# Mixture-of-experts tail of a fused block: 45 slots of 128 rows become 25 full slots and 14 slots shared by two experts

## The reference, cut to what matters

```python
# x, ctx: (32, 128, 256) f32; 16 heads of 16; 14 experts; hidden width 512
x = x + tanh(g_xattn) * attention(layernorm(x), ctx, ctx)     # causal, biases on q, k, v and dense
h = layernorm(x).reshape(4096, 256)
logits = h @ router_w                                         # (4096, 14)
e = argmax(logits); weight = softmax(logits)[e]
hid = gelu(h @ w1[e] + b1[e])                                 # (512,)
x = x + tanh(g_ffn) * weight * (hid @ w2[e] + b2[e])
```

## Time and profile before

| | |
|---|---|
| median of three runs | 489.14 us (488.89 to 490.43) |
| profiled execution, its own time | 491.46 us |
| its span | 489.6 us |
| busy in the span: TensorE, its weight loads, VectorE, ScalarE, GpSimd | 96%, 83%, 70%, 64%, 65% |
| mean granted TensorE clock | 0.991 of full speed |
| moved by DMA | 73.05 MB |

### The profile page before, as it was taken

How to read it: one execution, slowest core, us unless ns; L and a number is a source line. 1 busy time by engine, 2 the same in 40 slices (tenths; PEclk the granted TensorE clock), 3 DMA queues, 4 the chain that set the end, 5 groups by cost and what they waited for, 6 DMA issues and landing times.

```text
span 489.6 us, 17052 instructions
## 1 busy us (share of the span) xinstructions
PE 471.0 (96%) x4871; PEld 408.1 (83%) x4872; DVE 344.8 (70%) x1108; ACT 312.6 (64%) x1450; POOL 317.3 (65%) x686
## 2 busy tenths in 40 slices
PE   8999999999999999999999998989899999999991
PEld 4888888888888888888888887879799999999991
DVE  3678999999999999999999997654344334334431
ACT  2589899889898898898898897442222332233230
POOL 5465577686776777777777676686655555655621
PEclk9899999999999999999999999999999999999997
DMA  7264565312312212213111057598988888878810
GB/s 232 75 236 142 168 196 158 72 52 57 75 44 60 69 43 70 59 46 83 44 56 55 26 170 220 155 241 289 293 265 279 264 271 281 286 262 264 269 39 0
DMA packets 37904, 73.05 MB, mean 149 GB/s; under 512 B 12761, under 2 KB 21471, under 8 KB 37856
## 3 DMA queue, kind: packets, MB, share of 16 engines
q1 hardware_dynamic: 24752, 32.13, 22.8%
q10 hardware_dynamic: 6048, 23.54, 14.9%
q0 software_dynamic: 7056, 16.79, 11.1%
HBM read 59.06 MB, written 15.07 MB: 151 GB/s over the span
## 4 chain that ended last, share of the span: by engine, by line
PE 74%; ACT 7%; DVE 5%; DMA 4%; issue 3%; POOL 2%; SPq 1%; ACTq 0%; POOLq 0%; DVEq 0%
PE bank L1323 14%; PE bank L1314 14%; PE bank L1354 10%; PE bank L1423 9%; ACT arena L760 7%; PE bank L1413 5%; PE bank L1346 5%; PE bank L1491 5%; PE bank L1362 4%; DMA g_rows<-token_rows,fetch_idx 3%; PE bank L1301 2%; PE bank L1409 2%; DVE negmax L982 2%; PE bank L1341 2%; DMA arena<-ctxt 2%
## 5 line engine op out<-in xcount | busy, mean ns | idle before, releaser
L760 ACT ACTIVATE arena<-bank,negmax 128x128 f32<-128x128 f32 x512 | 179.6, 403 | 13.4 <-DVE negmax L982 13.4
L744 ACT ACTIVATE hid_t<-bank,w_ring 128x128 f32<-128x128 f32 x180 | 51.3, 369 | 114.5 <-PE bank L1314 90.2
L760 ACT ACTIVATION_READ_ACCUMULATOR arena<-bank,negmax 128x1 f32 x512 | 124.1, 242 | 0.0
L982 DVE TENSOR_REDUCE negmax<-bank 128x4 f32<-128x512 f32 x128 | 84.6, 683 | 9.6 <-PE bank L1346 8.9
L1314 PE MATMUL bank<-g_xt,w_ring 128*128 128x128 f32 x720 | 87.9, 275 | 0.6 <-DVE g_xt L955 0.6
L1323 PE MATMUL bank<-W,hid_t 128*128 x360 | 85.4, 380 | 1.6 <-ACT hid_t L744 0.8
L1314 PEld LDWEIGHTS bank<-g_xt,w_ring 128*128 128x128 f32 x720 | 84.6, 192 | 1.5 <-issue 1.0
L971 DVE SCALAR_TENSOR_TENSOR g_out<-bank,g_name,g_out 128x256 f32<-128x256 f32 x45 | 21.8, 484 | 86.5 <-PE bank L1323 86.5
L1354 PE MATMUL bank<-C,arena 128*128 128x128 f32 x512 | 78.9, 277 | 2.5 <-ACT arena L760 1.9
L1323 PEld LDWEIGHTS bank<-W,hid_t 128*128 128x128 f32 x360 | 65.0, 190 | 9.4 <-issue 2.4
L1423 PE MATMUL bank<-arena 128*128 128x128 f32 x512 | 71.5, 283 | 0.5 <-DMA arena<-ctxt 0.3
(11 more groups left out here) (151 smaller groups left out, 774.4 us busy)
## 6 DMA issues: line engine op xcount, KB each, us to landing
w_ring<-w1b ACTq DMA_DIRECT2D x35, 642.0 KB, 5.0
token_rows<-rows SPq DMA_DIRECT2D x32, 256.0 KB, 3.6
W<-w SPq DMA_DIRECT2D x14, 512.0 KB, 4.9
w_ring<-w1b SPq DMA_DIRECT2D x10, 642.0 KB, 7.2
arena<-x SPq DMA_DIRECT2D x32, 128.0 KB, 2.0
arena<-ctxt SPq DMA_DIRECT2D x31, 128.0 KB, 2.7
slot_names<-token_names SPq DMA_DIRECT2D x45, 1.0 KB, 4.6
g_rows<-token_rows,fetch_idx POOLq DMA_INDIRECT x45, 4.5
```

The lines of the kernel that those rows point to most:

```text
L744: ins = act.activation(hid_t[:, RING[k], ch, :], hid_bank[k][:, ch * P:(ch + 1) * P], ACT.Gelu, bias=w_ring[:, k, B1_AT + ch:B1_AT + ch + 1])
L760: ins = act.activation(probs[:, q, v, :], bank[q][:, v * P:(v + 1) * P], ACT.Exp, bias=negmax[:, b.par, h:h + 1], accum_out=rsum[:, b.par, ...
L982: dve.tensor_reduce(negmax[:, b.par, q * HQ:(q + 1) * HQ], bank[q][:, :].rearrange("p (v k) -> p v k", v=HQ), axis=AX_X, op=ALU.max, negat ...
```

## The change: full and mixed slots

A slot still has 128 rows, but there are 25 full ones (`FULL`) for one expert each, and then 14 mixed ones (`MIXED`), 39 in all. In mixed slot j, rows 0 to 63 are a half of any expert (from a table), and rows 64 to 127 are the last half tile of expert j, the same for every run.

- In a mixed slot the tokens are stationary and the weights move. `half_up`: for each of 2 chunks, one matmul of 64 stationary columns and 512 moving ones for the upper half (weights in `w_ring`) and one for the lower half (weights in the new resident `W1`), into partitions 0 to 63 and 64 to 127 of bank 5. `hidden` copies the bank (128 x 512) to `u_sb`, `turn` transposes it (4 transposes), `half_gelu` is 8 activations of 64 columns, `half_down` 4 x 2 matmuls of 64 stationary and 256 moving columns.
- `W1`, 512 KB for each of 14 experts, takes the place of the attention's buffers; SyncE loads it between slots 5 and 30 (`load_resident`). `load_half` issues three transfers for a mixed slot instead of one. Names of a mixed slot come in two transfers.
- `normed_rows` is gone from every batch step. `rows` holds 256 values, mean and reciprocal deviation (258 floats), and is stored when `rstd2_ready` is given. VectorE normalises gathered rows (`norm`, one slot further ahead than `up_in`), and `up_in` reads `g_xn`.
- The tables: `remaining_tiles` counts half tiles (6 linked operations where there were 2), and `take_full`, `half_tiles`, a second `place` and `half_lines` follow slots 11 to 14.
- The hardware loops over slots are written out, so all indices and waits there are constants.

```diff
-SLOTS = (TOK - E) // P + E
+HALF = P // 2
+MIXED = E
+FULL = (TOK // HALF - 1 - MIXED + 1) // 2
+SLOTS = FULL + MIXED
-ROW = 2 * D
+ROW = D + 2
...
+            def load_resident(e, behind):
+                hold(base_ready, behind)
+                sp.dma_start(W1[:, e, :], w1b[e, :, 0:DC * F]).then_inc(resident_loaded[e], 16)
...
+            load_resident(0, 5)
             for r in range(4):
                 hold(name_stored[r], 16 * (B // 4) + 16)
             hold(tables_ready, 2)
+            for s in range(EARLY, FULL):
+                hold(names_loaded[s % R], 16 * (s // R))
+                load_names(s % R, s)
+            load_resident(1, 9)
+            load_resident(2, 12)
+            load_resident(3, 15)
+            hold(tables_ready, 3)
+            for s in range(FULL, SLOTS):
+                hold(names_loaded[s % R], 16 * transfers(s - R, 2))
+                load_half_names(s % R, s)
+            for e in range(4, E):
+                load_resident(e, 18 + 2 * (e - 4) if e < 7 else 17 + e)
...
+            def load_half(r, s):
+                j = s - FULL
+                ex = act.value_load(half_expert[0:1, j:j + 1], min_val=0, max_val=E - 1)
+                weights = w1b[bass.ds(ex, 1), :, :].rearrange("e p n -> (e p) n")
+                act.dma_start(w_ring[:, r, 0:B2_AT], weights[:, 0:B2_AT]).then_inc(up_loaded[r], 16)
+                act.dma_start(w_ring[0:HALF, r, B2_AT:UPW], weights[0:HALF, B2_AT:UPW]).then_inc(up_loaded[r], 16)
+                act.dma_start(w_ring[HALF:P, r, B2_AT:UPW], w1b[j, HALF:P, B2_AT:UPW]).then_inc(up_loaded[r], 16)
...
+            def half_in(s):
+                half_gelu(s)
+                if s + R < SLOTS:
+                    hold(hid_t_ready, s + 1)
+                    hold(base_ready, s + 1)
+                    load_half(s % R, s + R)
...
+            def norm(r, s):
+                dve.wait_ge(rows_fetched[r], s // R * 16 + 16)
+                wait(dve, gx_transposed, s - 1)
+                dve.tensor_scalar(g_xn[:, RING[r], :], g_rows[:, r, 0:D], g_rows[:, r, MEAN:RSTD], g_rows[:, r, RSTD:ROW],
+                                  ALU.subtract, ALU.mult).then_inc(gx_normed, 1)
...
+            def full_slot(s):                      # VectorE
+                start_out(s % R, s)
+                up((s + 2) % R, s + 2)
+                norm((s + 3) % R, s + 3)
+                if s == FULL - 2:
+                    hidden(FULL)
+                    up((s + 3) % R, s + 3)
+                result(s % R, s)
+            def mixed_slot(s):                     # VectorE
+                if s + 3 < SLOTS:
+                    norm((s + 3) % R, s + 3)
+                start_out(s % R, s)
+                if s + 2 < SLOTS:
+                    hidden(s + 2)
+                if s + 3 < SLOTS:
+                    up((s + 3) % R, s + 3)
+                result(s % R, s)
...
-            def normed_rows(h):
-                normed(h, rows[:, h.slot, 0:D], rows[:, h.slot, D:2 * D], moments2, rstd2, rstd2_ready, h_ready)
...
             for s in range(4, EARLY):
+                norm((s + 3) % R, s + 3)
                 result(s % R, s)
...
+            def half_up(s):
+                j = s - FULL
+                pe.wait_ge(gx_ready, s + 1)
+                wait(pe, hidden_ready, j)
+                pe.wait_ge(up_loaded[s % R], 16 * transfers(s, 3))
+                pe.wait_ge(resident_loaded[j], 16)
+                for ch in range(DC):
+                    cols = slice(ch * F, (ch + 1) * F)
+                    pe.matmul(bank[5][0:HALF, :], g_xt[:, RING[s % R], ch, 0:HALF], w_ring[:, s % R, cols],
+                              start=(ch == 0), stop=(ch == DC - 1))
+                    ins = pe.matmul(bank[5][HALF:P, :], g_xt[:, RING[s % R], ch, HALF:P], W1[:, j, cols],
+                                    start=(ch == 0), stop=(ch == DC - 1))
+                ins.then_inc(half_hid_done, 1)
+            def half_down(s):
+                pe.wait_ge(hid_t_ready, s + 1)
+                pe.wait_ge(out_ready, s - 1)
+                ex = pe.value_load(half_expert[0:1, s - FULL:s - FULL + 1], min_val=0, max_val=E - 1)
+                for ch in range(FC):
+                    pe.matmul(y_bank[s % R][0:HALF, 0:D], hid_t[:, RING[s % R], ch, 0:HALF],
+                              W2[:, bass.ds(ex, 1), ch, :].rearrange("p e n -> p (e n)"),
+                              start=(ch == 0), stop=(ch == FC - 1))
+                    ins = pe.matmul(y_bank[s % R][HALF:P, 0:D], hid_t[:, RING[s % R], ch, HALF:P], W2[:, s - FULL, ch, :],
+                                    start=(ch == 0), stop=(ch == FC - 1))
+                ins.then_inc(y_done, 1)
+            def mixed_slot(s):                     # TensorE
+                if s + 2 < SLOTS:
+                    half_up(s + 2)
+                if s + 1 < SLOTS:
+                    turn(s + 1)
+                if s + 3 < SLOTS:
+                    up_in((s + 3) % R, s + 3)
+                if s < FULL:
+                    down(s % R, s)
+                else:
+                    half_down(s)
```

More of the change, by code:

```diff
@@ L1228, in _ @@
             row_moments(batch(30))
+            norm(2, 2)
             up(2, 2)
@@ L1243, in _ @@
             up(3, 3)
-            start_out(1, 1, 0)
+            start_out(1, 1)
             choose(last)
+            norm(4, 4)
             result(1, 1)
-            normed_rows(last)
             up(4, 4)
-            start_out(2, 2, 0)
+            start_out(2, 2)
             take_early()
@@ L1270, in _ @@
             up(1, EARLY + 1)
-            with dve.Fori(2, SLOTS // R - 1) as i:
-                for k in range(R):
-                    slot(k, i * R + k, i)
-            for k in range(R):
-                slot(k, SLOTS - R + k, SLOTS // R - 1, ahead=k + 2 < R)
+            for s in range(EARLY, FULL - 1):
+                full_slot(s)
+                if s == EARLY + 1:
+                    take_full()
+                if s == EARLY + 2:
+                    half_tiles()
+                if s == EARLY + 3:
+                    place(t_key_base, HALF)
+                if s == EARLY + 4:
+                    half_lines()
+            for s in range(FULL - 1, SLOTS):
+                mixed_slot(s)
         @block.tensor
@@ new lines, in full_slot @@
+            def full_slot(s):
+                up_in((s + 2) % R, s + 2)
+                up((s + 1) % R, s + 1)
+                if s == FULL - 2:
+                    half_up(FULL)
+                    up_in((s + 3) % R, s + 3)
[6 more added lines that the diff above has]
+                if s + 3 < SLOTS:
+                    up_in((s + 3) % R, s + 3)
+                if s < FULL:
+                    down(s % R, s)
+                else:
+                    half_down(s)
```

322 lines of the change are left out of this document (192 added, 130 removed).

## The result

The kernel before measured 489.25 us (median of 8, 488.44 to 491.34), the changed kernel 485.93 us (median of 8, 484.69 to 489.22). The ratio is 0.9921, 95% interval 0.9896 to 0.9946: 3.3 us less, where 7.8 us less was forecast. The time lies inside the range. The profiled execution of the changed kernel has a span of 484.0 us and an own time of 485.86.

What follows compares the result with a forecast made beforehand. TensorE, busy 96% of the span, was taken as the bound. 489.6 - 74.8 (full slots) + 62.6 (mixed slots) + 0.5 (end) + 1.5 (DMA) + 2.5 (joint) = 481.9 us span; median 0.46 below, 481.4 us; range 475 to 490.

Steps and rivals of the forecast that it cites:

- the mixed slot: TensorE's time for one slot of two halves, 4.47 us; 14 of them 62.6 us.
- the step that everything hung on: In `half_up` and `half_down`, both column groups work at once, so each takes 1.73 us, half of 3.46.
- both rivals on overlap: Mixed slots: groups overlap only in part, 490.4 us, chance 0.05; or not at all, 530 us, chance 0.03.
- ScalarE and the gathers stay hidden in the mixed slots: ScalarE occupied 4.4 of 4.47 us, gathers landing in time; rivals: gathers pace, 486, chance 0.12; ScalarE paces, 497, 0.08.
- the transfers: Slower loads and gathers around slots 24 to 31, charged 1.5 us in all.
- a burst: Residents 4 to 8 load together at slots 23 to 25; slots 24 to 31 run at over 300 GB/s.
- the joint: Between attention and expert slots, charged 2.5 us, bounds -2 and +6; a joint costing 6 us or more, chance 0.04.
- the norms ahead of `up_in`: VectorE in the joint: 0.4 us for each norm ahead of `up_in(2)` and `up_in(6)`.
- the gather of slot 10: In the joint, landing after 5.9 us, it delays `result(7)`, `base_ready(8)` and `down(9)` by about 1.2 us.
- the tail: Expert slots after the joint: 74.8 us leave, 62.6 come, plus 1.5 for DMA and 0.5 at the end.
- the reference: Sum starts from the earlier kernel's profiled span, 489.6 us; the median of runs taken as 0.46 below the span.

Runs made afterwards that it cites:

- `halves_in_turn`: Changed kernel with each mixed slot's matmuls ordered by half, all of the upper group first, then the lower: 494.24 us, ratio 1.0085 to the kernel before.
- `mixed_only`: Changed kernel's 25 full and 14 mixed slots, but rows normalised in batches and gathered with 2 KB as before: 489.03 us, ratio 0.9866; again 489.99 us, 0.9867.
- `before_third`: The kernel before, unchanged, run once more for a further profile on another chip: 491.92 us (one run).
- version with three edits: Changed kernel with norm(0, 5) ahead of the tables, early slots' norms behind the result, and `W1` loads spread between loads of names: 481.61 us, ratio 0.982.
- `loops_written_out`: The kernel before with its five hardware loops over slots written out and nothing else: 496.67 us, ratio 0.996.
- `before_again`: The kernel before, unchanged, run for a second profile: 498.59 us.
- padded kernels: The kernel before with 60 idle semaphore increments on VectorE, ScalarE and SyncE ahead of the attention loop, run twice: 491.48 us, ratio 1.0041; 491.08 us, ratio 1.0016.
- `norm5_residents`: Changed kernel with norm(0, 5) ahead of the tables and `W1` loads spread between the loads of names: 482.77 us, ratio 0.9852.
- `norm_only_again`: Second run of the kernel before with all 45 slots full and only the change to normalising gathered rows: 495.82 us, ratio 0.9996.

## Why the prediction was wrong, point by point

**Right: the mixed slot.** 4.40 us in most of them against 4.47. `half_up` and `half_down` keep a pair every 0.43 and 0.22 us, so the step that everything hung on, read from `attend`, holds; both rivals on overlap are out for this order of instructions. The Trainium skill (TensorE: Matmul & The Clock Gate, Packing small matmuls) has matmuls in strict order. The trace of `halves_in_turn` differs, and it decides: the record at 417.12 started ahead of three that stand before it in the order, the first of them at 417.33. Full slots stay at 3.73.

**Right: ScalarE and the gathers stay hidden in the mixed slots.** The three issues of `load_half` usually take 0.34, 0.50 and 0.63 us of the queue (the second took 1.33 and 1.35 in two loads), the eight activations 1.75 (1.9 forecast), and TensorE never waits for `hid_t` there, nor for a gather after slot 24.

**Right in place, a little low: the transfers.** Charged with 1.5 us; the burst of residents cost one wait of 2.1. It came in slot 28, while ten residents were on the queue; a burst was forecast, for slots 24 to 31. From 416 to 430 us DMA moved 376 GB/s, with a share that the profile gives as 1.03.

**Wrong: the joint, 5.3 us instead of 2.5.** This is the term that failed. From start to start of TensorE's `up` groups, in us:

```
                          before   changed   difference
up(1) to up(2)              7.62      7.51      -0.1
up(2) to up(3)              3.80      4.93      +1.1
up(3) to up(4)              4.37      4.31      -0.1
up(4) to up(5)              4.33      9.26      +4.9
up(5) to up(6)              6.19      3.84      -2.4
up(6) to up(9)             11.19     11.19       0.0
up(9) to up(11)             9.46     11.19      +1.7
```

It was mis-sized in three parts. For `norm(0, 5)` nothing was charged, and this is the largest: that the norm of slot 5 stands behind the whole chain of tables (320.31 to 322.98 us) was not followed on VectorE's timeline. It cost 2.74 us of waiting and 1.8 of half clock behind it. The half clock had no place in the sum at all: the trace of before has full clock in the joint, where its longest wait is 1.38 us. One slot later 2.4 us come back, as `up_in(6)`, which had waited 1.38 us for its gather with 0.53 of issue behind it, now waits for nothing.

The second part is the norms ahead of `up_in`. The sum had 0.4 each for slots 2 and 6, and neither shows as a loss. It shows at slot 3 instead, where `up_in(3)` waits 0.40 for its norm and 0.32 follow as issue; `up(2)` to `up(3)` is 1.1 us longer. Every kernel of this study with gathered norms has the same 4.93 there, and both runs of `mixed_only` the 3.80 of before.

For the gather of slot 10 the mechanism was right and stated (it delays `result(7)`, `down(9)` and the rest); it was sized with 5.9 us to land and took 7.63, so 1.7 us rather than 1.2. In the other profile without holds and with the same joint (`halves_in_turn`) it took 6.09, and the joint cost 3.1 us against `before_third`.

**Wrong by 1.5 us: the tail**, 8.6 us of gain instead of 10.2. The mixed slots gave back 1.0 us, at 4.40 instead of 4.47. The waits of 2.1 us for weights and 0.7 us of issue at the end are against 1.5 + 0.5. That leaves about 1.7 us for the rest, in single rows that the sum had no term for; 0.3 of it is one slot behind the second group of table matmuls (373 us). With the residents spread the tail is 127.7 and 127.8 us in two kernels: 10.5 and 10.4 gained.

**Off by chance, and both ways: the reference.** The sum was made against a profiled execution of the kernel before whose attention ended 2 us late, and "the median lies 0.46 below the span" was taken over to a kernel whose median lies 1.9 above its span. The first put the forecast 2.2 us too late, the second 2.4 us too early; they cancel, which is luck. The joint and the tail together were forecast 4.3 us too short.

**The gain was there.** 8.6 us come out of the tail, 5.3 are given back in the joint; 3.3 remain. The version with three edits has 48.8 us in the joint, 1.1 over `before_third`, and measured 481.6 us, where the forecast said 481.4. (These come from different sets; the ratio is 0.982, and 0.984 was forecast.) So the lost part lies mostly in the order of instructions and transfers in the joint, and not in the mixed slots.

**Left open.** What the holds are. They are not an effect of the hardware loops being written out (`loops_written_out` and `before_again` have them alike), and the joint is nearly as long with them in every kernel, whatever its order of work. They are not waits for data alone, as SyncE's late register instructions wait for nothing; late delivery of instructions would fit that, but no run here tests it. Two records of the instruction queue stand near them (322.7 and 341.6 us in `before_again`), but the first profile has two as well, at 322.3 and 334.8, without a hold. The padded kernels were made for this question, and both fell on chips without holds.

## What to carry to other kernels

When work is moved from a hidden loop to a joint, follow every moved instruction down its engine's own list and name what it now stands behind: here three places in the joint took back 5.3 of the 8.6 us that 14 shared slots brought. Add to the price of a long gap in TensorE's work what may follow it at half clock: 1.8 us behind the 2.74 here. And taking away one wait is worth nothing while the next transfer in the chain keeps its date: `norm5_residents` lost at slot 9 what it won at slot 5, and the joint shrank only in the version that also has the norms behind the result.

## What the runs showed of the hardware

- Two column groups of 64 ran fully side by side in f32 where their matmuls alternate: a pair every 0.43 us at 512 columns, 0.22 at 256. With one group's eight records first (`halves_in_turn`), four went alone; the other group started 0.92 us behind the first, while three records ahead of it still waited, and kept that lag: 5.31 us a slot instead of 4.40.
- TensorE's granted clock fell behind the waits of 2.74 (changed kernel), 3.05 (`norm5_residents`) and 4.14 us (`before_again`), to between 0.50 and 0.81 in the windows behind them, and a group there took 3.58, 3.22 and 3.75 us instead of 1.73 to 1.79. The length of the wait alone does not decide it: behind 2.07 us in `norm_only_again` the next `down` took 3.49, and behind 2.45 us in the changed kernel it took its usual time.
- On two of the chips VectorE and ScalarE stand still together for 3 to 6 us (ScalarE up to 9.6 us) in the joint, in all 12 profiles taken there, for a cause that the trace does not show, and register instructions of SyncE come up to 1.4 us late. The kernel before takes 496 to 499 us there and 489 to 490 elsewhere, and the change's gain is 0.8% in one set and 2.3% in another.
- Beside ten transfers of 512 KB issued in 26 us on SyncE's queue, three transfers of 642 KB together, issued from 415.98 to 417.01 on ScalarE's, landed at 428.84, 12.9 us after the first issue, where one transfer of 642 KB had taken 4.6.
